# x loaded into another buffer four positions earlier, matmuls reordered, and a coupling update split in halves

## The reference

```python
xi, res = split(x @ W_in.T + b_in)            # 512 channels each
xi = silu(causal_conv4(xi) + b_conv)
delta, B, C = split(xi @ W_x.T + b_x)         # delta = softplus, 512; B and C 16 each
h_t = exp(delta*A) * h_(t-1) + delta * B * xi # scan over tokens, 512 channels x 16 states
y = sum_n(h*C) + xi*D
x1 = layernorm(x + (y * silu(res)) @ W_out.T + b_out)
gf = tanh-like global factor of mean(x1)      # 256 -> 128 -> 64 -> 1
out = x1
for _ in range(3):                            # 256 -> 256 -> 128 -> 64 -> 1, GELU between
    tf = sigmoid(coupling_net(out))
    out = out + (0.1 + range*(0.7*gf + 0.3*tf - 0.5)*2) * twist(out)
result = layernorm(x1 + out)
```

## Time and profile before

| | |
|---|---|
| median of 3 runs | 4038.7 us (4038.14 to 4043.2) |
| profiled execution, its own time | 4040.28 us |
| its span, first to last instruction | 4038.5 us |
| granted TensorE clock, mean | 0.946 |
| POOL busy | 90% of the span |
| PE, DVE, ACT busy | 87%, 85%, 73% |
| DMA | 630.04 MB, mean 156 GB/s |

### The profile page before, as it was taken

One profiled execution on the slowest core, in us unless ns is written; L12 is line 12 of the kernel. 1 busy time (PEld: TensorE's weight loads), 2 busy tenths in 40 slices (PEclk: granted clock), 3 DMA queues, 4 the chain that ended last, 5 costly groups with the idle time before them and its releaser, 6 DMA issues. The chain is left out here.

```text
span 4038.5 us, 51729 instructions
## 1 busy us (share of the span) xinstructions
PE 3524.4 (87%) x18776; PEld 1611.5 (40%) x18776; DVE 3429.6 (85%) x2508; ACT 2959.0 (73%) x3918; POOL 3644.6 (90%) x1604
## 2 busy tenths in 40 slices
PE   7669989899998998989898998989989898897766
PEld 3224353443434344353443434344353443434233
DVE  4988988889898898989889898898989889898861
ACT  4447868778786877868777786877868777785753
POOL 4999999999999999999999999999999999999860
PEclk9779999999999999999999999999999999998888
DMA  5354373543536354373644546454363544546320
GB/s 182 130 175 154 128 230 120 188 152 130 186 130 224 129 191 138 122 229 120 197 148 155 159 152 200 140 187 129 133 218 123 194 149 158 160 138 199 127 86 31
DMA packets 329645, 630.04 MB, mean 156 GB/s; under 512 B 27952, under 2 KB 226608, under 8 KB 329136
## 3 DMA queue, kind: packets, MB, share of 16 engines
q1 hardware_dynamic: 329392, 626.74, 47.0%
HBM read 456.76 MB, written 169.87 MB: 155 GB/s over the span
## 5 line engine op out<-in xcount | busy, mean ns | idle before, releaser
L1060 POOL TENSOR_TENSOR work<-u_q,b_quad 128x1024 f32<-128x1024 f32 x1024 | 2397.3, 2372 | 138.2 <-DMA u_q<-u_scratch 97.1
L816 ACT ACTIVATE da<-delta_q,neg_a 128x1024 f32<-128x1024 f32 x1024 | 1126.3, 1112 | 600.9 <-DVE work L995 430.8
L987 DVE TENSOR_TENSOR_SCAN da<-da,work 128x1024 f32<-128x1024 f32 x608 | 1389.9, 2286 | 151.4 <-ACT da L816 119.7
L1067 POOL TENSOR_TENSOR work<-work,c_quad 128x1024 f32<-128x1024 f32 x416 | 985.2, 2368 | 11.6 <-DVE work L987 11.3
L987 DVE TENSOR_TENSOR_SCAN work<-da,work 128x1024 f32<-128x1024 f32 x416 | 945.9, 2278 | 29.9 <-ACT da L816 28.1
L727 PE MATMUL y_sum<-work,v_all 128*32 128x256 f32 x8192 | 613.3, 399 | 303.3 <-POOL work L1067 190.7
L995 DVE TENSOR_TENSOR work<-da,c_quad 128x1024 f32<-128x1024 f32 x608 | 743.9, 1224 | 28.6 <-DMA c_quad<-bc_scratch 4.6
L752 ACT ACT_TABLE_LOAD x563 | 722.3, 1283 | 14.5 <-DMA v_all<-in_vectors 3.9
L727 PEld LDWEIGHTS y_sum<-work,v_all 128*32 128x32 f32 x8192 | 199.8, 110 | 771.0 <-issue 259.3
L613 PE MATMUL banks<-xi,w_all 128*128 128x512 f32 x1024 | 479.8, 612 | 9.4 <-ACT g_act L797 5.1
L600 PE MATMUL banks<-xi,taps 128*128 128x512 f32 x984 | 453.2, 606 | 0.0
(11 more groups left out here) (86 smaller groups left out, 3270.3 us busy)
## 6 DMA issues: line engine op xcount, KB each, us to landing
delta_q<-delta_scratch SPq DMA_DIRECT2D x256, 512.0 KB, 5.8
u_q<-u_scratch SPq DMA_DIRECT2D x256, 512.0 KB, 6.1
delta_scratch<-delta SPq DMA_DIRECT2D x64, 512.0 KB, 2.9
u_scratch<-soft SPq DMA_DIRECT2D x64, 512.0 KB, 2.9
b_quad<-bc_scratch SPq DMA_DIRECT2D x64, 512.0 KB, 4.7
c_quad<-bc_scratch SPq DMA_DIRECT2D x64, 512.0 KB, 7.1
s_quad<-res_scratch SPq DMA_DIRECT2D x128, 256.0 KB, 4.1
y_scratch<-s_quad SPq DMA_DIRECT2D x128, 256.0 KB, 3.2
```

The source lines that it names most:

```text
L816: act.activation(da[:, t % 2, :], delta_q[:, slot, :], ACT.Exp, scale=neg_a[:, t % PERIOD:t % PERIOD + 1]).then_inc(da_ready, 1)
L987: dve.tensor_tensor_scan(dst, da[:, t % 2, :], work[:, slot, :], 0.0, ALU.mult, ALU.add) \
L1060: pool.tensor_tensor(work[:, slot, :], u_q[:, copied, :], b_quad[:, j, :], ALU.mult) \
L1067: pool.tensor_tensor(work[:, un % WORK, :], work[:, un % WORK, :], c_quad[:, un % PHASE, :], ALU.mult) \
```

## The change

`x_res` becomes a view of `x1`, so x is loaded into `big`. The load stands at position 62 and waits for the last "e" block of the batch before; for batch 0 it waits for the two stores of first gates that lie in `big`. ACT's first write of a transposed block to `oT` gets the wait for "out". In "o" and "e" the matmuls whose data are early come first, and the wait for the late data stands behind them in the first half block. The coupling update on POOL is done for each half of the tokens, with a wait and a signal for each, and the first-layer matmuls of the next cycle wait for their half. All other positions stay.

```diff
-XRES_AT = 66
+XRES_AT = 62
-        x_res = oT[:, :, :].rearrange("p m t -> p (m t)").rearrange("p (k c) -> p k c", c=DM)
+        x_res = x1
                 if (f := batch_at(t, XRES_AT)) is not None:
                     if f == 0:
-                        sp.wait_ge(first_stored[DC - 1], 64)
+                        sp.wait_ge(first_stored[1], 64)
+                        sp.wait_ge(first_stored[2], 64)
                     if f:
-                        for h in range(2):
-                            sp.wait_ge(out_done[h], 32 * f)
+                        sp.wait_ge(e_ready, 4 * f)
                     sp.dma_start(x_res, x[f].rearrange("(k p) c -> p k c", p=P)).then_inc(xr_in, 16)
...
                 if kind == "o":
-                    pe.wait_ge(yg_in[n % 2], 64 * (2 * f + n // 2 + 1))
                     if n == 0:
                         pe.wait_ge(xr_in, 16 * (f + 1))
                     for r in range(2):
                         tb = 2 * n + r
                         half = shared[:, r * DM:(r + 1) * DM]
+                        pe.matmul(half, eye, x_res[:, tb, :], start=True, stop=False)
+                        pe.matmul(half, eye, b_out, start=False, stop=False)
+                        if r == 0:
+                            pe.wait_ge(yg_in[n % 2], 64 * (2 * f + n // 2 + 1))
                         for k in range(4):
-                            pe.matmul(half, yg[:, n % 2, k, r * P:r * P + P], w_out[:, k, :], start=k == 0, stop=False)
-                        pe.matmul(half, eye, b_out, start=False, stop=False)
-                        mm = pe.matmul(half, eye, x_res[:, tb, :], start=False, stop=True)
+                            mm = pe.matmul(half, yg[:, n % 2, k, r * P:r * P + P], w_out[:, k, :],
+                                           start=False, stop=k == 3)
...
                 elif kind == "e":
                     pe.wait_ge(re_in, 16 * (f + 1))
-                    pe.wait_ge(f_prod, 2 * (CYCLES * f + CYCLES - 1) + n // 2 + 1)
...
                         pe.matmul(half, eye, residual[:, tb, :], start=True, stop=False)
                         for m in range(2):
                             pe.matmul(half[:, m * P:m * P + P], oT[:, m, tokens], eye, start=False, stop=False)
+                        if r == 0:
+                            pe.wait_ge(f_prod, 2 * (CYCLES * f + CYCLES - 1) + n // 2 + 1)
+                        for m in range(2):
                             mm = pe.matmul(half[:, m * P:m * P + P], big[:, 1 - m, tokens], minus if m else eye,
                                            start=False, stop=m == 1)
...
-                            pe.wait_ge(updated, (CYCLES - 1) * f + c)
+                            pe.wait_ge(updated, 2 * ((CYCLES - 1) * f + c - 1) + half + 1)
...
                             act.wait_ge(t_ready, 4 * f + n + 1)
+                            if n == 0 and f:
+                                for h in range(2):
+                                    act.wait_ge(out_done[h], 32 * f)
...
-                            pool.wait_ge(f_prod, 2 * cycle + 2)
-                            pool.tensor_tensor(oT[:, 0, :], oT[:, 0, :], big[:, 1, :], ALU.add)
-                            pool.tensor_tensor(oT[:, 1, :], oT[:, 1, :], big[:, 0, :], ALU.subtract).then_inc(updated, 1)
+                            for half in range(2):
+                                cols = slice(half * L, half * L + L)
+                                pool.wait_ge(f_prod, 2 * cycle + half + 1)
+                                pool.tensor_tensor(oT[:, 0, cols], oT[:, 0, cols], big[:, 1, cols], ALU.add)
+                                pool.tensor_tensor(oT[:, 1, cols], oT[:, 1, cols], big[:, 0, cols], ALU.subtract) \
+                                    .then_inc(updated, 1)
```

## The result

| | before | after |
|---|---|---|
| median of 5 runs | 4038.14 us (4037.52 to 4043.2) | 4058.33 us (4055.34 to 4063.29) |
| ratio, 95% interval | | 1.0045 [1.0034, 1.0056] |
| span of the profiled execution | 4038.5 us | 4056.5 us |
| granted TensorE clock, mean | 0.946 | 0.942 |

The kernel became slower by 0.45%, where 0.28% had been forecast. The span splits at two places that both traces have: the landing of the last b_quad load of the last boundary, and the last store of y, with which the tail begins.

The account below looks back on a forecast made before the run. The prediction took GpSimd (POOL), busy 3644.6 of 4038.5 us, to set the pace. From 4040.3 us, +25.5 at the boundaries and -14.6 in the tail gave 4051.2, or 4049.6 against the median; 80% range 4024 to 4078.

Parts of the forecast that it names:

- Place and sign of the loss: At batch boundaries, x queued ahead of the last b_quad load lengthens POOL's wait for it, a loss reaching the end.
- 1.7 us per boundary, 25.5 in all: Delay of the last b_quad load behind x at 15 batch boundaries, +25.5 us (7 to 44).
- the rival that the hole swallows x: At the 15 boundaries, 2.2 us of free DMA time absorbs x: price 0, kernel 4024 us; chance 0.2.
- the prediction's queue: At a boundary, landings reckoned in issue order: x 2.7 us, c_quad and b_quad 1.3 each, b_quad 2.1 us late.
- estimate of 4.0 us per boundary: At each boundary, the skill page's 6.15 us for 1 MB less the 2.2 us hole; kernel 45 us net lost.
- Steady order and halves at nothing: In steady running, reordered matmuls cost 0; 60 extra POOL instructions, covered by its waits, cost 0 (0 to 11 us).
- The tail: Batch 15's coupling, with nothing beside it, becomes shorter: -14.6 us (5 to 16).
- "o" starts earlier, first half block shorter: In the tail, "o" waits for yg rather than x, with early matmuls ahead of the wait: -7.0 us (4.5 to 7.5).
- two updates: In the tail, TensorE starts after half 0 of each coupling update: 3.3 us, twice, -6.6 us (0 to 7).
- "e": In the tail, the residual and oT matmuls of "e" go ahead of the wait: -1.0 us.
- the 0.7 us for yg loads without x's traffic around them: In the tail, part of the gain at "o": x's traffic gone from around the yg loads, some 0.7 us more.
- the sum: Whole kernel: +25.5 us at the boundaries and -14.6 in the tail, +10.9 on the span.

Follow-up runs that it names:

- e1: The changed kernel with the x load back at position 66 instead of 62; ratio 0.9979 to the kernel before.
- e2: The kernel before with only the x load changed (into big, at position 62, with its waits), matmul order and whole updates kept; ratio 1.0048 to the kernel before.
- e7: The changed kernel, x at 62, with the last b_quad load moved from position 63 to 60, ahead of x; ratio 0.9887 to the kernel before.
- e10: The kernel of e1 (x load at 66) with SP's wait for the last "e" block still at position 62; ratio 0.9977 to the kernel before.
- e9: The kernel before with only the matmul order of "o" and "e" changed, as in the change; ratio 1.0000 to the kernel before.
- e3: The kernel before with only the coupling updates done by halves; ratio 0.9987 to the kernel before.
- e11: e7 with extra matmuls of unused result in TensorE's idle places of the last batch's coupling; ratio 0.9880 to the kernel before.

## Why the prediction was right, and where its terms were off

**Place and sign of the loss: right.** POOL's wait for b_quad, x ahead of c_quad in the queue, landing in the order of issue, SP not held: all as forecast. e1 and e2 show the place, e7 the order in the queue, and e10 that SP was not held. What had been lost at the boundaries reached the end in full (the stretch from the last b_quad landing to the y store is 231.20 us in both). TensorE's waits for x, 16.1 us from 284 to 3728 us before, are gone.

**1.7 us per boundary, 25.5 in all: measured 27.8. Right in size, in part by luck.** The 14 later boundaries lost 24.13 us, 1.72 each; the first lost 3.67. Such a figure scatters from one execution to the next: the first landing was at 297.6 to 300.3 us in the runs with x at 66, and the batch took 240.65 to 241.66. The timed runs put it at 1.6 to 2.0 us: e2 is 0.48% (19.4 us) slower with a tail 5.1 us shorter, which leaves 24.5 for 15 boundaries, and the change is 0.66% (26.7 us) slower than e1 with a tail 2.7 us shorter, which leaves 29.4. The reckoning by the queue was good: x takes 2.95 us, not 2.7, behind the load before it, and pushes b_quad that far back, but c_quad and b_quad then land closer together: b_quad came 1.95 us after c_quad in the emptier queue, and 1.26 us after it now. That slack of 0.7 us, which the prediction (with 0.6) gave to the rival that the hole swallows x, is real; it shortens the delay and does not cancel it. What is left is 2.2 us, and 7.7 less 5.5 from issue to landing is the same; the prediction's queue gave 2.1. It then took 1.7, because the hole is not at one place, and that step is not borne out: the wait grew by 2.1 us for each boundary.

That the span lost only 1.72 for each of the 14 later ones has another reason. Over these 14 batches the b_quad waits grew by 27.6 us (23.7 to 51.3, the first boundary left out), the halves added 7.2 us of POOL's busy time, and POOL's other waits shrank by 10.7, which makes 24.1. In e2, which has no halves, the waits grew by 27.5 us and the batches by 27.3: there b_quad's delay cost nearly all of itself, as the prediction had said. Why the other waits shrank by as much as they did is open. So the 1.7 and the 1.72 agree partly by luck.

The Trainium skill, page "DMA: Bandwidth & Descriptors", section "Bandwidth", gives 6.15 us for a transfer of 1 MB, issued from GpSimd there. The trace does not bear out adding that price behind a full queue, where x took 2.95 us, and the estimate of 4.0 us per boundary made from it was more than twice what was lost. The same page's section "Queues, rings and completion order" lets a later descriptor finish writing first. The loads of 0.5 and 1 MB at the boundaries landed in the order of issue, but the traces also agree with the page: in the tail of the kernel before, a yg load issued 0.8 us after x (3913.54 and 3912.73) landed 0.5 us ahead of it (3919.60 and 3920.07).

**Steady order and halves at nothing: right, within what the runs can tell.** e9 gives 1.0000 for the order, e3 no loss for the halves in the timed runs. A half took 1.26 us, as forecast (1.28), and the next one starts 1.22 us after it (3993.69 to 3994.91), where the two whole instructions of before started 2.30 us apart (3970.68 to 3972.98). Twice 1.22 less 2.30 is 0.14 us for each extra instruction, not 0.19. POOL's busy time agrees: it rose by 7.2 us for 56 extra instructions in 14 batches, 0.13 each. e1, with the same halves and x at 66, has batches no longer than before (240.68 us), so in that trace the time lies in what POOL would have waited; in the profiled trace of e3 it does not, and only the interval of e3's ratio speaks against a cost of 8 us.

**The tail, -14.6 forecast, -9.75 measured.** By terms:

| term | forecast us | measured us |
|---|---|---|
| "o" starts earlier, first half block shorter | -7.0 | -4.6 |
| two updates | -6.6 | -6.6 (3.27 and 3.29) |
| "e" | -1.0 | -0.9 |
| TensorE at the 1.2 GHz level for longer | not in the sum | +2.4 |

*The "o" term was mis-sized*, by 2.4 us in three parts. First, "o" came 3.74 us closer to the y store, not 4.6. The third of the four yg issues lasted 1.65 us instead of 0.49, so the fourth load went out 6.9 us after the store instead of 5.7 and landed at 3944.22, just before the first matmul on it. What lengthened that issue is open, and it is not a fixed price of the change: with x at the same place the first matmul on yg stands 9.15 us after the store in e2 and 9.12 in e7, 4.8 us closer, a little more than the forecast. The x load does stand ahead of the y store now, by 2.6 us (3931.41 and 3934.03), and the store landed 4.3 us after its issue instead of 2.2, but this held back the first yg load by only 0.2 us (4.34 instead of 4.16 after the store), since the four stores of "out" are issued in between. Second, the matmuls moved ahead of the wait gave 1.68 us, but 0.79 went back, since the second half of the block was still at the 1.2 GHz level. Third, the 0.7 us for yg loads without x's traffic around them did not appear in this trace.

*The clock was the term left out.* TensorE's idle places in the tail became shorter and lie elsewhere, and the low stretches lie on other work. After the second update the 16 matmuls took 10.10 us instead of the 8.54 of before, 1.56 us; a new low stretch at 3970.5 cost the "t" and first-layer matmuls 0.96. e11 tests whether filled idle places change this: against e7, the two first-layer groups after the updates became 3.8 us shorter together, and of three low stretches of about 3, 10 and 7 us between "o" and the last matmul one of about 3 us was left. That the clock decided the 2.4 us of the change itself is read from the trace's lengths, not from a run that held everything else still; e7 has the same groups in 9.62 and 10.15 us, so they are not a chance of one execution.

**Size.** The two misses add up: 2.3 us more lost at the boundaries and 4.9 less won in the tail make 7.2 of the span, +18.0 where the sum said +10.9. They are small beside the 25.5 and 14.6, but not beside their difference.

## What to carry to other kernels

Ask of a load that is issued earlier not whether its own wait goes away, but what stands behind it in the queue and who waits for that: here a wait of TensorE of 1.7 us that cost nothing was exchanged for some 1.9 us (27.8 over 15) at each boundary on the engine that sets the pace. Order a queue by due time and not by readiness: moving the 0.5 MB load that is waited for ahead of x took the changed kernel from 0.45% slower to 1.1% faster than the kernel before, and with x out of the way that move alone was worth 0.56%. Do not read a cause from one long issue or one slow batch of one trace; look whether the other runs with the same code have it. In a serial tail, count each gain with the engine's clock as the trace grants it there, since a step that comes earlier may run at the lower level.

## What the runs showed of the hardware that was not expected

- The spacing of two 0.5 MB loads differed with what was ahead of them: b_quad landed 1.95 us behind c_quad with a hole in the DMA engines' work, 1.26 us with the queue full.
- A later transfer can land first on one queue: a yg load (128 KB) issued 0.8 us after x (1.05 MB) landed 0.5 us ahead of it. The loads of 0.5 and 1 MB at the boundaries kept their order.
- One DMA issue of SP in the tail took 1.65 us where the same issue took 0.49 before, and it held back the start of "o" by about 1 us.
- 1.05 MB of x took 2.95 us of a full queue in 1 KB pieces and 2.51 us in 8 KB pieces (medians over the boundaries).
- The effect of bytes in front of an awaited load was not linear: +9.0 us of waits for half of x, +31.0 for all of it.
- Splitting a GpSimd operation of 128x1024 into two of 128x512 cost 0.13 to 0.14 us.
- Extra matmuls in idle places shortened a chain of TensorE's work: 16 matmuls in 7.13 us instead of 10.15 (e11 and e7).
